# Counts in both column halves, one bias matmul a group, and a blend from -h in a two-layer graph network

## What is computed

```python
# layer 0: mean of the edge features of each destination, a linear map, softplus
sums = segment_sum(edge_feats, dst); counts = segment_sum(ones, dst)
mean_edge = sums / maximum(counts, 1.0)
h0 = concat([x, mean_edge, global]) @ W.T
x = layernorm(x + softplus(h0) - log 2)
# layer 1: an edge weight out of the rows of both ends, a weighted sum, a gate
h = relu(ln(x @ W1 + b1) * g1 + bt1)
w = sigmoid(relu(concat([h[src], h[dst]]) @ We1 + be1) @ We2 + be2)
aggr = segment_sum(w * h[src], dst)
gate = sigmoid(concat([h, aggr]) @ Wg + bg)
h_new = gate * aggr + (1 - gate) * h
out = layernorm(x + ln(h_new) * g2 + bt2)
```

## Time and profile before

| what | value |
|---|---|
| median of three executions | 2209.81 us |
| the profiled execution | 2215.08 us |
| its span | 2213.3 us |
| stage A, first to last pair | 33.5 to 404.5 us |
| stage B, first `mean_mm` to the last full `dst_mm` copied | 407.1 to 556.8 us |
| stage C, the gathers and their steps | 557 to 2117 us |
| stage D | 2117.9 to 2213.3 us |
| busy: PE, DVE, ACT, POOL | 1594.7, 1670.4, 1187.7, 1434.0 us |
| chain that ended last | POOL 45%, PE 22%, issue 19%, DVE 7% of the span |

### The profile page before, as it was taken

The page is one execution under the profiler, slowest core; times in us unless marked ns, Lnnn a source line. Parts: engine busy times, 40 slices in busy tenths (PEclk is TensorE's granted clock), DMA queues, the critical chain, the costliest instruction groups (busy, mean ns, idle before and its releaser), DMA issues.

```text
span 2213.3 us, 44515 instructions
## 1 busy us (share of the span) xinstructions
PE 1594.7 (72%) x13238; PEld 1420.5 (64%) x13239; DVE 1670.4 (75%) x7154; ACT 1187.7 (54%) x3254; POOL 1434.0 (65%) x1437
## 2 busy tenths in 40 slices
PE   4999896898456467777777777777676668766770
PEld 3777775686456456777767677777666667766740
DVE  7666776585799568888888887888877777777766
ACT  1455553465677046665566665666655544545325
POOL 4354430142677777777777777777777777777765
PEclk9999999677566557777777777778778886788675
DMA  7888898114544545555565566666666666666401
GB/s 274 267 289 285 298 320 281 36 43 136 173 141 138 159 127 174 167 175 178 162 178 171 162 186 186 175 194 182 182 187 190 180 186 187 189 181 197 129 3 58
DMA packets 279085, 394.19 MB, mean 178 GB/s; under 512 B 75155, under 2 KB 178612, under 8 KB 278715
## 3 DMA queue, kind: packets, MB, share of 16 engines
q1 hardware_dynamic: 217155, 226.47, 32.3%
q0 software_dynamic: 57408, 156.84, 24.1%
q10 hardware_dynamic: 4280, 8.03, 1.1%
HBM read 376.07 MB, written 15.12 MB: 177 GB/s over the span
## 4 chain that ended last, share of the span: by engine, by line
POOL 45%; PE 22%; issue 19%; DVE 7%; ACT 3%; DMA 2%; DVEq 1%; ACTq 1%; SPq 0%; POOLq 0%
POOL x_rows L897 33%; POOL ring L897 11%; PE bank L495 7%; PE bank L1307 3%; PE bank L502 2%; PE bank L542 2%; ACT ring L998 2%; DMA x_rows<-src_table,lane_src 2%; DVE bank L531 2%; PE bank L1279 1%; PE bank L1410 1%; PE bank L1249 1%; DVE sums L1835 1%; PE bank L1316 1%; PE bank L1309 1%
## 5 line engine op out<-in xcount | busy, mean ns | idle before, releaser
L897 POOL DMA_INDIRECT x_rows<-src_table,lane_src x900 | 887.8, 986 | 301.2 <-issue 270.9
L531 DVE SCALAR_TENSOR_TENSOR bank<-bank,we_all 128x128 f32<-128x128 f32 x1686 | 431.3, 323 | 11.2
L897 POOL DMA_INDIRECT ring<-src_table,lane_src x296 | 289.9, 979 | 90.2 <-issue 88.1
L546 DVE TENSOR_TENSOR sums<-sums,bank 128x128 f32 (+1 forms) x814 | 206.3, 253 | 186.5 <-issue 105.7
L1116 ACT ACTIVATE ring<-sums,be_all 128x4 f32<-128x4 f32 (+1 forms) x124 | 36.9, 297 | 511.9 <-DVE bank L531 511.9
L527 DVE TENSOR_TENSOR bank<-bank,x_rows 128x512 f32<-128x512 f32 x225 | 146.3, 695 | 204.6 <-DMA x_rows<-src_table,lane_src 204.3
L1387 PE MATMUL bank<-ring,sums 128*128 128x128 f32 x980 | 265.1, 359 | 45.2 <-DVE bank L531 44.3
L522 PE MATMUL bank<-ring,onehot_t 120*128 120x128 bf16 x1196 | 133.8, 279 | 183.3 <-issue 126.9
L542 PEld LDWEIGHTS bank<-weighted,x_rows 128*128 128x128 f32 x1800 | 259.7, 229 | 0.0
L542 PE MATMUL bank<-weighted,x_rows 128*128 128x40 f32 x1800 | 258.2, 311 | 0.0
L1365 PE MATMUL bank<-sums 128*128 128x98 bf16 (+1 forms) x736 | 93.1, 298 | 203.6 <-issue 139.4
(11 more groups left out here) (252 smaller groups left out, 3356.3 us busy)
## 6 DMA issues: line engine op xcount, KB each, us to landing
ring<-in_edge_attr SPq DMA_DIRECT2D x195, 512.0 KB, 4.8
ring<-rel_table SPq DMA_DIRECT2D x74, 512.0 KB
ring<-cell_table SPq DMA_DIRECT2D x121, 256.0 KB
ring<-src_table SPq DMA_DIRECT2D x144, 128.0 KB
x_rows<-src_table,lane_src POOLq DMA_INDIRECT x900
ring<-dst_table SPq DMA_DIRECT2D x299, 32.0 KB
ring<-src_table SPq DMA_DIRECT2D x104, 64.0 KB
src_table<-ring SPq DMA_DIRECT2D x12, 512.0 KB, 3.7
```

The source lines that it names most:

```text
L531: last = eng.scalar_tensor_tensor(hid[:, j, :], hid[:, j, :], 0.0, wide["we2"][:, :], ALU.max, ALU.mult, accum_out=out[:, j:j + 1])
L546: return eng.tensor_tensor(table[..., bass.ds(start, width)], table[..., bass.ds(start, width)], part, ALU.add)
L897: eng.indirect_dma_start(gathered(c)[:, j, :], None, src_table, bass.IndirectOffsetOnAxis(ap=lane_src[:, t:t + 1], axis=0)).then_inc(gathe ...
```

## The change

1. `edge_counts`: the four count matmuls have 64 columns of ones as weights, and j even goes to columns 0 to 63, j odd to 64 to 127. Each half holds the counts of half of the edges.
2. After the last sum SyncE loads row 0 and row 64 of the counts into a small tile, 49 rows of 128 each; two matmuls with parts of the identity turn and add them for all blocks at once, in `mean_mm(0)`. The 49 matmuls of single elements go, and `pre_` takes the maximum and reciprocal once.
3. `add_bias`: one bias matmul of up to 512 columns for a group, ahead of the block matmuls, in `xw`, `w1_mm` and `dst_mm`.
4. `scalar_hot` goes; VectorE makes the one-hots of all pairs.
5. `aggr` starts from -h, written by GpSimd (`less_h`, stage 9), in place of `blank`. `apart` goes, and `wg_h` becomes `wg_h` + `wg_a`.

```diff
         def edge_counts(eng, out, hots):
             for j in range(J):
-                last = eng.matmul(out, ones_b[:, :], half[:, :, j, :, 1], start=(j == 0), stop=(j == J - 1), skip_group_check=True)
+                last = eng.matmul(out[j % 2 * W0:(j % 2 + 1) * W0], ones_b[:, 0:W0], half[:, :, j, :, 1],
+                                  start=(j < 2), stop=(j >= J - 2), skip_group_check=True)
...
+            eng.wait_ge(done("acc_all"), 1)
+            for v in range(2):
+                eng.dma_start(count_rows[v * n_blocks:(v + 1) * n_blocks, :],
+                              sums[v * W0:v * W0 + 1, 1, 0:padded].rearrange("a (b r) -> a b r", r=P)).then_inc(done("count_rows"), 16)
...
+            def less_h(g):
+                need(eng, "mean_mm", g)
+                need(eng, "h_cols", g)
+                eng.tensor_scalar(aggr[:, block_cols(g)], h_cols[:, block_cols(g)], -1.0, None, ALU.mult).then_inc(done("less_h"), 1)
...
+            eng.tensor_tensor(wg_h[:, :], wg_h[:, :], wg_a[:, :], ALU.add)
+            run_stages(n_groups, [(2, residual), (NORM2_AT, gain), (NORM2_AT + 3, less_h)])
...
-            def apart(g):
-                cols = block_cols(g)
-                need(eng, "mix_mul", g - 2)
-                eng.tensor_tensor(soft[:, g % 2, 0:blocks_of[g] * P], aggr[:, cols], h_cols[:, cols], ALU.subtract).then_inc(done("apart"), 1)
-                eng.tensor_tensor(y1[:, g % 2, 0:n], soft[:, g % 2, 0:n], pre[:, g % 2, 0:n], ALU.mult).then_inc(done("mix_mul"), 1)
-            run_stages(n_groups, [(1, mix_mul), (0, apart)])
+                eng.tensor_tensor(y1[:, g % 2, 0:n], aggr[:, block_cols(g)], pre[:, g % 2, 0:n], ALU.mult).then_inc(done("mix_mul"), 1)
+            for g in range(n_groups):
+                mix_mul(g)
...
-                if q + HOT_PAIRS in scalar_hots:
-                    scalar_hot(q + HOT_PAIRS)
...
+            def add_bias(out, nb, which):
+                eng.matmul(out[:, 0:nb * P].rearrange("p (b f) -> p b f", b=nb), ones_b[0:PARTS, :],
+                           bias_parts[:, which, :].unsqueeze(1).to_broadcast([PARTS, nb, P]), start=True, stop=False, skip_group_check=True)
...
-                for b in range(g * GB, g * GB + blocks_of[g]):
-                    last = eng.matmul(count_out[:, b:b + 1], sums[0:1, 1, b * P:(b + 1) * P], ones[0:1, 0:1],
-                                      start=True, stop=True, skip_group_check=True)
-                last.then_inc(done("count_mm"), 1)
                 per_block(g, bank[0], lambda b: sums[:, 0, (g * GB + b) * P:(g * GB + b + 1) * P], w_edge[:, :]).then_inc(done("mean_mm"), 1)
+                if g == 0:
+                    loaded(eng, "count_rows", 2)
+                    for v in range(2):
+                        last = eng.matmul(count_out, count_rows, ident[0:2 * n_blocks, v * n_blocks:(v + 1) * n_blocks],
+                                          start=(v == 0), stop=(v == 1), skip_group_check=True)
+                    last.then_inc(done("count_mm"), 1)
...
-                if q in scalar_hots:
-                    eng.drain()
-                    eng.sem_inc(done("hot"), 1)
-                    return
...
-            def blank(g):
-                need(eng, "mean_mm", g)
-                eng.memset(aggr[:, block_cols(g)], 0.0)
```

More of the change, by code:

```diff
@@ L187, in gnn_pair @@
         weighted = sb("weighted", [P, 3, 2, J, W])
+        assert 2 * n_blocks <= P and P <= 2 * J * W
+        count_rows = weighted[0:2 * n_blocks, 0, :, :, :].rearrange("p c j w -> p (c j w)")[:, 0:P]
         pad_rows = sb("pad_rows", [(dst_rows - padded) * PARTS, P], BF16)
@@ L623, in sort_hot @@
             return rows_[:, sort_order[q] % 2, :, :, :], cols_[:, sort_order[q] % 2, :, :]
-        scalar_hots = [q for q in range(SCALAR_HOTS + 3, n_pairs) if q % SCALAR_HOTS == 3]
         def pair_sums_of(c):
@@ L876, in gain @@
                 eng.tensor_tensor(z, z, wide["bt1"][:, :].unsqueeze(1).to_broadcast([P, nb, P]), ALU.add).then_inc(done("offset"), 1)
+            def less_h(g):
+                need(eng, "mean_mm", g)
+                need(eng, "h_cols", g)
+                eng.tensor_scalar(aggr[:, block_cols(g)], h_cols[:, block_cols(g)], -1.0, None, ALU.mult).then_inc(done("less_h"), 1)
             loaded(eng, "small", N_SMALL)
             loaded(eng, "x_rows", 2 if tail_nodes else 1)
-            run_stages(n_groups, [(2, residual), (NORM2_AT, gain)])
+            eng.tensor_tensor(wg_h[:, :], wg_h[:, :], wg_a[:, :], ALU.add)
+            run_stages(n_groups, [(2, residual), (NORM2_AT, gain), (NORM2_AT + 3, less_h)])
             eng.wait_ge(done("mean_mm"), n_groups)
@@ L990, in xw_out @@
                                bank[4 + g % 2][:, 0:nb * P], ACT.Copy).then_inc(done("xw"), 1)
[L992 to L998, removed]
-                eng.drain()
-                flat = hots.rearrange("p c j w -> p (c j w)")
-                eng.activation(flat, flat, ACT.Relu, bias=ones[:, 0:1], scale=-1.0).then_inc(done("scalar_hot"), 1)
             for q in range(n_pairs):
@@ L1245, in xw @@
                 need(eng, "xw", g - 2)
+                add_bias(bank[4 + g % 2], nb, 2)
                 for b in range(nb):
@@ L1248, in xw @@
                     n0 = (g * GB + b) * P
-                    eng.matmul(o, h_cols[:, n0:n0 + P], w_node[:, :], start=True, stop=False)
-                    last = eng.matmul(o, ones_b[0:PARTS, :], bias_parts[:, 2, :], start=False, stop=True)
+                    last = eng.matmul(o, h_cols[:, n0:n0 + P], w_node[:, :], start=False, stop=True, skip_group_check=True)
                 last.then_inc(done("xw_mm"), 1)
@@ L1258, in pair_mm @@
                 need(eng, "hot", q)
-                if q in scalar_hots:
-                    need(eng, "scalar_hot", scalar_hots.index(q))
                 need(eng, "pair_rows", q - 2)
@@ L1300, in per_block @@
             def per_block(g, out, lhs, rhs, added=None, turn=False):
+                if added is not None:
+                    add_bias(out, blocks_of[g], added)
                 for b in range(blocks_of[g]):
@@ L1306, in per_block @@
                     else:
-                        last = eng.matmul(o, lhs(b), rhs, start=True, stop=added is None)
-                        if added is not None:
-                            last = eng.matmul(o, ones_b[0:PARTS, :], bias_parts[:, added, :], start=False, stop=True)
+                        last = eng.matmul(o, lhs(b), rhs, start=added is None, stop=True, skip_group_check=added is not None)
                 return last
@@ L1711, in pre_ @@
             def pre_(g):
[L1713 to L1716, removed]
+                if g == 0:
+                    need(eng, "count_mm", 0)
+                    step(eng.tensor_scalar(inv_count[:, :], count_out, 1.0, None, ALU.max))
+                    step(eng.reciprocal(inv_count[:, :], inv_count[:, :]))
                 need(eng, "mean_mm", g)
@@ L1797, in _ @@
                 (4, norm1), (1, pre_), (2, soft_sum), (3, moments1_), (NORM2_AT, norm2), (5, moments2_),
-                (DST_AT + 1, rest_), (DST_AT + 2, part2), (3, blank)])
-            eng.drain()
+                (DST_AT + 1, rest_), (DST_AT + 2, part2)])
+            eng.wait_ge(done("less_h"), n_groups)
             if columns > padded:
@@ L1985 @@
 REL_AT = 2
-SCALAR_HOTS = 4
 NORM2_AT = 6
```

3 lines of the change are left out of this document (removed).

## The result

The kernel after takes 2176.42 us, the median of four runs (2170.79 to 2178.69), against 2209.57 for the kernel before beside it: a ratio of 0.9844 with a 95% interval of 0.9825 to 0.9864. The forecast was 2165 with a range of 2140 to 2190. The time fell inside it, 11 us above the forecast.

The account below looks back on a forecast made before the run. TensorE was taken to lead stages A and B, GpSimd's gathers stage C. Stages A, B and D gave -16 - 22 - 7 = -45 us on the profiled 2215.1; less 5.3 to the median, 2165 us, range 2140 to 2190.

Parts of the forecast that it names:

- I take 0.12: Stage A, TensorE: overlapping counts save 0.12 of their 0.24 us a pair, 24 us over 196 pairs.
- 64 ns each: Stage A, TensorE: the sums, 16 instructions in two array halves, take 1.03 us; nearest row for the counts' overlap.
- Stage A, xw: TensorE's xw: with one wide bias a group falls from 2.3 to 1.7 us, 7 us over 12 groups.
- these 28: Stage A: 28 us lost between coupled engines today (371 against 343), kept on top of 327 to give 355 us.
- VectorE becomes the bound: Stage A: VectorE's 327 us, with the added one-hots, exceed TensorE's 312; the stage takes 355 us, 16 less.
- The rival that VectorE swallows the gain: Stage A stays within 3 us of 371, the run takes 2184 us; chance 0.19.
- ScalarE's relief: Stage A: ScalarE loses nine instructions in each of 48 pairs, ahead of copies TensorE waited for; part of the 28 us.
- Step 0: Stage B, first step: pre_(0) waits for two small loads, then two matmuls follow; 1 us more.
- steps 1 to 3: Stage B: a loop of mean_mm and pre_, 5.15 us long, loses 1.8 us a step, 5 us in all.
- From step 4 on VectorE's work sets the step: Stage B: without memset, maximum, reciprocal and some waiting, 13 steps lose 1.2 us each, 15 us.
- the cover of less_h: Stage B: GpSimd's 23.92 us wait for src_table hides less_h's 13 instructions of some 1.3 us each.
- The signs: Listed observations: right if counts-to-turn is 0.12 us and mixed stage B steps 6 to 7; wrong if stage A's clock is low.

Follow-up runs that it names:

- a_hots4: Kernel after with part 4 undone: ScalarE makes the one-hot of every fourth pair again; 2176.4 us, ratio 0.9860 to the kernel before.
- a_turnhalf: Kernel after with the turn of pair rows as two 64-column matmuls in place of one transpose; 2168.0 us, ratio 0.9816 to the kernel before.
- a_pieces: Kernel after with GpSimd's two widest ranking operations cut into three each; 2413.6 us, ratio 0.9829 to the kernel before, beside it at 2454.3.
- a_apart: Kernel after with part 5 undone: blank and apart back, less_h gone; 2186.0 us, ratio 0.9897 to the kernel before.
- a_bias: Kernel after with part 3 undone: a bias matmul for each block again; 2431.2 us, ratio 0.9900 to the kernel before, beside it at 2454.3.
- the first two sets: Two of three sets of four follow-up kernels; the kernel before, timed beside each, took 2211.5 and 2208.6 us, and 2454.3 in the third.

## Why the prediction was right or wrong

**The sign and the size** were right: faster, 2176 us in a range of 2140 to 2190, near the forecast's 2165. Of the 11 us between, 7 are the sum (-37.9 against -45), and 4.6 the step from the profiled execution to the median, for which I carried over the 5.3 us of before; that of after was 0.7. That it is so near is in part luck: stages A and B gave 25 us where 38 were forecast, and 5 of the 13 missing came back from stage D and from stage C, which the change doesn't touch.

**Stage A, TensorE's counts.** "I take 0.12" for the counts was right for themselves and wrong for the pair, which gained 0.07: the boundary where the tiling changes moved from before the counts to after them, at no cost, and the turn to the next sums takes 0.05 us more. The term was 24 us and measured 13.7 (196 x 0.07). The "64 ns each" of the sums had the boundary in it: without it they take 0.93 us, 58 ns each. The rule that I set against the change, from the section Restrictions of the Trainium skill's page TensorEngine Tiling (Array Packing), that column tiling disables the fast weight load, shows no price here: the four weight loads take 0.23 us in both kernels.

**Stage A, xw.** Sized too low. A group takes 1.41 us where nothing disturbs it (143.24 to 144.65), not 1.7, so 11 us of work went, not 7. With the counts that is 25 us of work, but TensorE's busy time fell by 16 only; the granted clock had gone from 0.98 to 0.93.

**Stage A, VectorE.** The terms came out: 283 us busy, 33.5 of register loads and 12 of the late loads are 328, said was 327. What is lost between the engines was 33 us (361 - 328), not "these 28": that is the 6 us by which the stage was missed. But the reading of the sum, "VectorE becomes the bound", failed. Taking 39 us of work off VectorE gave 1.9 us (a_hots4), taking 196 x 0.20 = 39 us off TensorE gave 11.6 (a_turnhalf), and cutting GpSimd's operations, which adds work, gave 7.5 (a_pieces). No engine's load sets this stage alone. Single stalls count beside it: three slots didn't cover a one-hot of 2.7 us, and a low clock followed the wait. The rival that VectorE swallows the gain was right in that a good part of it was lost, and wrong in why: the added one-hots cost nothing. That ScalarE's relief is a part of the gain was wrong too: a_hots4 shows the exchange to be even.

**Stage B.** Step 0 cost 1.9 us, not 1; steps 1 to 3 gave 4.2, not 5: 1.85 in each of the first two, 0.5 in the third. "From step 4 on VectorE's work sets the step" failed. The rest of the stage lost 13.9 us (129.7 to 115.8), not 18, and not where I put it: the memset traded against less_h is worth 0.8 us (a_apart), while part 3, TensorE's alone, is worth 10.3 (a_bias). The last steps follow the write of dst_table at 4.7 to 4.9 us, as said, and the cover of less_h held.

**Stage D** gave 9.4 us in the traces and 8.4 in a_apart, forecast 7: 2.16 us a group against 2.3. **Stage C** was left alone; its 3 us lie within the 1553 to 1562 us that it took in the kernels of the first two sets.

**The signs.** As said came: no L1316, one bias a group, 50 us of idle time ahead of the adds of VectorE, `rest_` every 4.7 to 4.9 us, 2.16 us in stage D. Not as said: from counts to turn 0.22 us, not 0.12; the steps with mean_mm, w1_mm and dst_mm in them took 6.9, 7.7 and 8.6 us, not 6 to 7 (moments2_ at 458.08, 465.03, 472.76 and 481.32); and the clock of stage A fell to 0.93, which I had named as a sign of being wrong.

**By part**, from the stages of the kernels that undo one: part 1 up to 6 us, part 2 6.9, part 3 12.1, part 4 nothing, part 5 9.2. That is 28 to 34, and the medians differ by 33. By the ratios it is coarser: parts 1 and 2 undone together cost 5.5 us (0.9869 against 0.9844, intervals that overlap), part 3 11.0, part 5 11.7, 28 in all.

## What to carry to other kernels

Cost a matmul that changes the array's tiling with its two boundaries and not by itself, and group work of one tiling, so that a boundary falls away rather than moves. In a ring of three slots look for the longest instruction of each engine rather than at the sum of its work, and for what GpSimd runs beside VectorE's: a delay longer than the ring holds is passed on, and in the one followed here the low clock after it cost as much again. To know which engine sets a step, undo the part that relieves it: in stage B the engine that I read off the timeline was not the one that paid.

## What the hardware showed

**VectorE behind GpSimd.** In stage A of the kernel after, 14 one-hots or scans took 1.37 to 2.80 us, and each lies beside one of GpSimd's operations of 1116 elements. VectorE's adds with one operand in PSUM kept to 0.29 us throughout. In stage D VectorE's sum went from 1.74 us, where GpSimd's two operations follow each other without a gap, to 0.66, where there is one with a gap behind it; the 1.74 end 0.55 us after `apart` in the earlier trace rows:

```profile
2135.28 1.74 DVE L1959 TENSOR_TENSOR sums<-ring,h_cols 128x512 f32<-128x512 f32 x1
```

```profile
2104.13 0.66 DVE L1952 TENSOR_TENSOR sums<-ring,h_cols 128x512 f32<-128x512 f32 x1
```

The Trainium skill's page SBUF — State Buffer, section SBUF: two separate sides, says that the two engines share a pair of ports as an exclusive lock that is held for the whole instruction, and that a VectorE operation with two SBUF inputs falls under it; the rows agree where GpSimd's operation has two inputs as well, in the ends of the long one-hots and in what cutting the operations into three did. They don't agree beside GpSimd's `tensor_scalar`, which has one:

```profile
119.08 3.90 POOL L828 TENSOR_SCALAR x_rows<-x_rows 128x372 bf16<-128x372 f32 x3
...
120.08 0.68 DVE L512 TENSOR_TENSOR ring<-iota,lane_dst 128x512 f32<-128x512 f32 x1
...
121.29 0.68 DVE L512 TENSOR_TENSOR ring<-iota,lane_dst 128x512 f32<-128x512 f32 x1
```

Two one-hots that began inside these operations took the 0.68 us of an undisturbed one.

**The clock after a wait.** After a wait of 2.27 us the sums ran at 1.97 us instead of 1.09, and the next xw at 2.08 instead of 1.16 us; the granted clock from 126.20 to 131.26 us was 0.50, the lower level of 1.2 GHz. From start to start these two and the next sums took 0.80, 0.93 and 0.65 us more than at the full clock, 2.4 together: the low clock cost as much again as the wait that came before it. After the wait of 0.82 us at 159.54 the sums kept to 1.09 us.

**Gathers that waited.** The three sets ran on three chips. In the last the gathers of the kernel after waited 184.5 us and 60.3 us for something that the profile calls remote, 244.8 together, in no trace of the first two sets, and stage C was 244.5 us longer; no other stage changed. The two numbers are not the same sum: other waits of the gathers changed too, the short ones for issue from 357 to 322 us. What the gathers waited for, and whether the chip is the reason, is not shown.
